# P V of four heads in four column strips, softmax sums from chunks added on GpSimd

## The reference, cut to what matters

```python
# first attention, per batch b
q, k = _rms_norm(q, g_q), _rms_norm(k, g_k)
logits = jnp.einsum('bhqd,bhkd->bhqk', q, k) * d ** (-0.5)
attn = jax.nn.softmax(logits, axis=-1)
o = jnp.einsum('bhqk,bhkd->bhqd', attn, v)
...
# second attention, causal
probs = jax.nn.softmax(scores, axis=-1)
out = jnp.einsum('bhqk,bkhd->bqhd', probs, v).reshape(b, s, H)
return out @ o_w
```

## Time and profile before

| | us |
|---|---|
| three runs | 1286.44, 1295.35, 1297.18 |
| median | 1295.35 |
| the profiled execution | 1290.86 |
| its span | 1289.1 |
| TensorE busy | 1169.7 |
| VectorE busy | 744.4 |
| ScalarE busy | 572.3 |
| GpSimd busy | 290.7 |

### The profile page before, as it was taken

One profiled execution on the slowest core, in us unless ns is written; L12 is line 12 of the kernel. 1 busy time (PEld: TensorE's weight loads), 2 busy tenths in 40 slices (PEclk: granted clock), 3 DMA queues, 4 the chain that ended last, 5 costly groups with the idle time before them and its releaser, 6 DMA issues.

```text
span 1289.1 us, 18670 instructions
## 1 busy us (share of the span) xinstructions
PE 1169.7 (91%) x6059; PEld 825.7 (64%) x6059; DVE 744.4 (58%) x1807; ACT 572.3 (44%) x1248; POOL 290.7 (23%) x244
## 2 busy tenths in 40 slices
PE   5979999999999889999999989989999999999970
PEld 5745555665566446557767757766657888888850
DVE  6565675477545856666565575566364774444433
ACT  3324464345443555455465454455264753222210
POOL 1313122100210031001011200200124464555530
PEclk9979999999999999999999999999899999999995
DMA  7064243125311732352284264265357744555559
GB/s 255 33 180 131 65 136 112 50 86 184 99 50 58 225 107 57 99 189 88 88 259 149 86 234 122 84 201 176 86 186 232 262 152 105 109 108 113 115 134 331
DMA packets 88127, 178.42 MB, mean 138 GB/s; under 512 B 12609, under 2 KB 23265, under 8 KB 86497
## 3 DMA queue, kind: packets, MB, share of 16 engines
q1 hardware_dynamic: 79216, 156.90, 37.4%
q0 software_dynamic: 8512, 19.93, 8.2%
...
...
## 4 chain that ended last, share of the span: by engine, by line
PE 77%; DVE 8%; DMA 5%; ACT 4%; issue 3%; SPq 1%; POOL 0%; DVEq 0%; ACTq 0%; POOLq 0%
PE psum L862 14%; PE psum L681 9%; PE psum L682 8%; PE psum L683 8%; PE psum L846 6%; PE psum L825 6%; PE psum L690 4%; PE psum L940 4%; PE psum L942 4%; PE psum L941 4%; PE psum L967 2%; PE psum L969 2%; PE psum L968 2%; PE psum L909 2%; PE psum L772 2%
## 5 line engine op out<-in xcount | busy, mean ns | idle before, releaser
L1174 ACT ACTIVATE probs<-psum 128x512 f32<-128x512 f32 (+3 forms) x512 | 257.3, 517 | 231.5 <-PE psum L849 120.6
L825 PE MATMUL psum<-stack 96*128 96x512 f32 (+3 forms) x512 | 210.2, 416 | 8.6 <-DMA stack<-split_s 4.0
L1583 DVE TENSOR_REDUCE nmax<-psum 128x1 f32<-128x512 f32 x256 | 170.5, 684 | 77.0 <-PE psum L825 73.2
L846 PE MATMUL psum<-stack 97*128 97x512 f32 (+3 forms) x512 | 197.3, 386 | 16.8 <-ACT probs L1174 15.4
L862 PE MATMUL psum<-probs,vals 128*33 128x512 f32 (+3 forms) x1024 | 209.4, 531 | 0.0
L1586 DVE CUSTOM_DVE_ANT_0 psum<-psum,causal 128x128 f32<-128x128 f32 (+3 forms) x256 | 123.0, 501 | 21.0 <-PE psum L825 19.4
L825 PEld LDWEIGHTS psum<-stack 96*128 96x128 f32 x512 | 100.0, 196 | 46.3 <-issue 23.7
L846 PEld LDWEIGHTS psum<-stack 97*128 97x128 f32 x512 | 99.0, 193 | 40.0 <-ACT probs L1174 25.8
L862 PEld LDWEIGHTS psum<-probs,vals 128*33 128x33 f32 x1024 | 49.8, 112 | 99.6 <-issue 65.5
L681 PE MATMUL psum<-w_hi,xh 128*128 128x512 f32 (+1 forms) x256 | 95.4, 373 | 4.2 <-DVEq L1449 2.5
L682 PE MATMUL psum<-w_hi,xl 128*128 128x512 f32 (+1 forms) x256 | 93.6, 366 | 0.0
...
...
## 6 DMA issues: line engine op xcount, KB each, us to landing
...
```

Source lines behind the costliest of these rows:

```text
L825: sq.filled(nc.tensor.matmul(psum[:, sq.bank(M), 0:n], st[:, 0, t * P:(t + 1) * P], st[:, 1, 0:n], start=True, stop=True), M)
L846: last = nc.tensor.matmul(psum[:, bank, lo:S], st[:, 1, t * P:(t + 1) * P], st[:, 0, lo:S], start=True, stop=not masked)
L1174: sk.cleared(nc.scalar.activation(probs[:, M % NX, lo:S], psum[:, sk.bank(M), lo:S], ACT.Exp, scale=SCALE), M)
L1583: sq.cleared(V.tensor_reduce(out, psum[:, sq.bank(M), :], AX.X, ALU.max, negate=True), M)
```

## The change

`VW`, the 33rd column and the pair's way back are gone. V is 32 columns wide, and `pv(Q, t)` issues, for four heads (a quad, 16 steps) and one chunk t, four products to partitions 0, 32, 64 and 96 of bank 7. The groups stand at steps 11, 12, 14 and 16 of the quad. GpSimd adds chunks 1 to 3 of each head onto the head's chunk 0, in place, after chunk 0 has been used (`add_probs`, at steps 11 to 19). At step 22 TensorE multiplies the four totals by a 128x32 block of ones, which repeats each sum on the 32 partitions of its head (`sum`). VectorE transposes that in 32x32 blocks, takes one reciprocal per query, transposes it back broadcast, and multiplies the P V bank by it into the sum's ring bank (`sum` in the VectorE list); ScalarE and VectorE split the result as before (`o`). There are 14 chunk slots, given out by a table (`SLOT`), and ScalarE waits for the last reader of the slot: a P V group and an add, or the ones product for chunk 0. `out` moves from steps 23 to 35 to 10 to 19 of the next block, the first `qk` from step 3 to 0, the others and `v` too; x1, residual and accumulator rows move in tiles of 128 tokens through a buffer of two tiles.

```diff
 NSTEPS = NB * STEPS_H
 LEAD = 16
 TURN_AHEAD = 5
-LAG = 2
-GROUP = 4
-NX = 2 * GROUP
+NX = 14
+PV_STEPS = (11, 12, 14, 16)
+SUM_STEP = 22
+ADDS = {11: ((0, 1), (1, 1)), 13: ((2, 1), (3, 1)), 14: ((0, 2), (1, 2)), 16: ((0, 3), (1, 3)), 17: ((2, 2), (3, 2)),
+        19: ((2, 3), (3, 3))}
+TAIL_STEPS = 8
...
     if i >= 0:
-        put((5,), [("back", i, NPR - 1)])
-        put((8,), [("turn_o", i, NC - 1)])
-        put((23, 27, 31, 35) if phase(j) == 1 else (25, 29, 33, 37), each("out", i, NT))
+        put((6,), [("sum", i, NQD - 1)])
+        put((8,), [("o", i, NQD - 1)])
+        put((10, 13, 17, 19), each("out", i, NT))
         if phase(i) == 2:
+            put((12, 15, 21, 23), each("acc", i, NT))
             put((28, 33, 36, 41), each("square2", i, NT))
             put((43, 43, 44, 44), each("norm2", i, 4))
-            put((47, 47, 49, 49), each("scale2", i, NT))
-            put((51, 52, 54, 55), each("x2", i, NC))
+            put((46, 46, 47, 47), each("scale2", i, NT))
+            put((49, 51, 52, 53), each("x2", i, NC))
             put((59, 62), each("router", i, 2))
...
     if j < NB and phase(j) == 1:
-        for n, m in enumerate((17, 18, 20, 21, 23, 24, 26, 27) if k == 0 else (3, 5, 7, 11, 13, 15, 19, 21)):
+        for n, m in enumerate((17, 18, 20, 21, 24, 25, 26, 27) if k == 0 else (0, 2, 4, 9, 12, 15, 20, 24)):
             put((m, m + 2), [("qk", j, n), ("hsum", j, n)])
-        put((30, 31, 32, 33) if k == 0 else (24, 25, 26, 27), each("hnorm", j, 4))
-        put((26, 30, 33, 39) if k == B - 2 else (39, 47, 55, 59), each("v", j, NT))
+        put((30, 31, 32, 33) if k == 0 else (27, 28, 29, 30), each("hnorm", j, 4))
+        put((26, 29, 32, 37) if k == B - 2 else (29, 32, 45, 52), each("v", j, NT))
         for g in range(NG):
-            late = 3 if k == 0 and g == 0 else 0
-            put((28, 29) if g == 0 and k else (33, 34) if g == 0 else (30 + 8 * g, 31 + 8 * g), hscales(j, g))
+            late = (3 if k == 0 else 2) if g == 0 else 0
+            put((33, 34) if g == 0 and k == 0 else (31, 32) if g == 0 else (30 + 8 * g, 31 + 8 * g), hscales(j, g))
             put((32 + 8 * g + late, 34 + 8 * g + late), turns(j, g))
     elif j < NB:
-        put((2, 5), [("kv_d", j), ("q_d", j)])
-        for n in range(2 * NT):
-            put((9 + 2 * n, 10 + 2 * n), [("qk", j, n), ("rope", j, n)])
-        put((27, 31, 35, 39), each("v", j, NT))
+        put((0, 2), [("kv_d", j), ("q_d", j)])
+        for n, m in enumerate((4, 9, 12, 15, 21, 24, 26, 28)):
+            put((m, m + 1), [("qk", j, n), ("rope", j, n)])
+        put((30, 33, 36, 45), each("v", j, NT))
         for g in range(NG):
             put((32 + 8 * g, 34 + 8 * g), turns(j, g))
...
         put((60, 61, 62, 63), each("x", after, NC))
-    put(range(13, 64, STEPS_P), each("back", k, NPR - 1))
-    put((38, 46, 57), each("turn_o", k, NC - 1))
+    put(range(SUM_STEP, 64, STEPS_Q), each("sum", k, NQD - 1))
...
+def step_of(Q, head, t):
+
+    return STEPS_Q * Q + STEPS_P * (head // 2) + 2 * t + head % 2
+
+
+def quad_part(M):
+
+    Q, m = divmod(M, STEPS_Q)
+    return Q, m // STEPS_P * 2 + m % 2, m % STEPS_P // 2
...
+def slots_of_probs():
+
+    add_step = {head_t: m for m, parts in ADDS.items() for head_t in parts}
+    slot_of, last, free_at = [], [None] * NX, [0] * NX
+    for M in range(NSTEPS):
+        s = min(range(NX), key=lambda n: free_at[n])
+        Q, head, t = quad_part(M)
+        slot_of.append((s, last[s]))
+        last[s] = (Q, head, t)
+        free_at[s] = STEPS_Q * Q + (SUM_STEP + 1 if t == 0 else max(PV_STEPS[t], add_step[head, t] + 1))
+    return slot_of
+
+
+SLOT = slots_of_probs()
...
         probs = rest("probs", [P, NX, S])
-        vals = [rest(f"vals{n}", [P, NT, H, VW]) for n in range(2)]
+        vals = [rest(f"vals{n}", [P, NT, H, DH]) for n in range(2)]
         vs = rest("vs", [P, 2, S])
         stack = rest("stack", [P, 2, NSTK, S], F32R)
+        spread = at("inverse_sums", rest.where, [P, NC, S])
         oh, ol = rest("o_hi", [P, NC, S], F32R), rest("o_lo", [P, NC, S], F32R)
-        oc = rest("o_chunk", [P, 2, NT, P])
-        ev = rest("o_pair", [P, 2, S])
...
-        yt = rest("yt", [P, NT, D])
+        ones_h = rest("ones_for_sums", [P, DH])
+        yt = rest("yt", [P, 2, D])
...
+            def store_x1(i, t):
+                ring.wait_read(sp, ("out", i, t))
+                sp.dma_start(x1_s[i][:, t, :], yt[:, t % 2, :]).then_inc(y1_st[t % 2], 16)
...
+                    if i >= 0 and phase(i) == 1 and m in (13, 16, 20, 22):
+                        store_x1(i, (13, 16, 20, 22).index(m))
+                    if i >= 0 and phase(i) == 2 and m in (14, 17, 24, 26):
+                        store_acc(i, (14, 17, 24, 26).index(m))
+                    if i >= 0 and phase(i) == 2 and m == 50:
                         store_x2(i)
...
-                elif kind == "back":
-                    p, = at_
-                    o.wait_read(pe, NPR * j + p)
+                elif kind == "sum":
+                    g, = at_
+                    Q = NQD * j + g
+                    pe.wait_ge(s_add, max(ADD_NO[Q, head, NT - 1] for head in range(HPG)) + 1)
                     ring.wait_free(pe, key)
-                    for t in range(NT):
-                        last = nc.tensor.transpose(psum[:, ring.bank(key), t * P:t * P + OW],
-                                                   ev[0:OW, p % 2, t * P:(t + 1) * P], ident[0:OW, 0:OW])
+                    for head in range(HPG):
+                        last = nc.tensor.matmul(psum[DH * head:DH * head + DH, ring.bank(key), :], ones_h[:, :],
+                                                probs[:, SLOT[step_of(Q, head, 0)][0], :], start=True, stop=True)
                     ring.filled(last, key)
-                elif kind == "turn_o":
-                    c, = at_
-                    for p in (2 * c, 2 * c + 1):
-                        ring.wait_read(pe, ("back", j, p))
-                    turn(key, lambda t: oc[:, c % 2, t, :])
                 elif kind == "out":
                     t, = at_
                     if t == 0:
-                        for c in (NC - 2, NC - 1):
-                            ring.wait_read(pe, ("turn_o", j, c))
+                        for g in (NQD - 2, NQD - 1):
+                            ring.wait_read(pe, ("sum", j, g))
...
-            def pv(M):
-                k, h, t = head_step(M)
-                p, side = M // STEPS_P, h % 2 * HALF
-                if M % STEPS_P == 0:
-                    o.wait_free(pe, p)
-                if M % STEPS_H == 0:
-                    for n in (NT - 2, NT - 1):
-                        ring.wait_read(pe, ("v", k, n))
-                sk.wait_read(pe, M)
+            def pv(Q, t):
+                k, g = divmod(Q, NQD)
+                if t == 0:
+                    pe.wait_ge(o_ok, Q)
+                    if g == 0:
+                        for n in (NT - 2, NT - 1):
+                            ring.wait_read(pe, ("v", k, n))
                 lo = t * P if phase(k) == 2 else 0
-                nc.tensor.matmul(psum[side:side + VW, o.bank(p), lo:S], vals[k % 2][:, t, h, :], probs[:, M % NX, lo:S],
-                                 start=(t == 0), stop=(t == NT - 1)).then_inc(pv_mm, 1)
+                for head in (HPG - 2, HPG - 1):
+                    sk.wait_read(pe, step_of(Q, head, t))
+                for head in range(HPG):
+                    nc.tensor.matmul(psum[DH * head:DH * head + DH, O_BANK, lo:S], vals[k % 2][:, t, HPG * g + head, :],
+                                     probs[:, SLOT[step_of(Q, head, t)][0], lo:S],
+                                     start=(t == 0), stop=(t == NT - 1)).then_inc(pv_mm, 1)
 
...
-            for M in range(NSTEPS + LAG):
+            for M in range(NSTEPS + TAIL_STEPS):
...
-                if (M - LAG) % GROUP == GROUP - 1 and M > LAG:
-                    for n in range(GROUP):
-                        pv(M - LAG - GROUP + 1 + n)
-                if M < NSTEPS:
                     for key in BESIDE[M // STEPS_H].get(M % STEPS_H, ()):
                         if key in RING_NO:
                             beside(key)
+                if pv_group(M) is not None:
+                    pv(*pv_group(M))
...
-                elif kind == "turn_o":
-                    c, = at_
-                    if j == 0 and c == 0:
-                        act.wait_ge(spare_set, 3 * 16)
-                    if j and c == 0:
-                        ring.wait_full(act, ("out", j - 1, NT - 1))
-                    hi_of(key, oh[:, c, :])
+                elif kind == "o":
+                    g, = at_
+                    act.wait_ge(o_ok, NQD * j + g + 1)
+                    copy(oh[:, g, :], psum[:, ring.bank(("sum", j, g)), :]).then_inc(hi_ok, 1)
...
-                if M >= NX:
-                    act.wait_ge(pv_mm, M - NX + 1)
+                slot, was = SLOT[M]
+                if was:
```

(75 more changed lines are left out.)

138 lines of the change are left out of this document (81 added, 57 removed).

## The result

The changed kernel takes 1385.3 us (median of 4 runs, 1382.7 to 1387.9) against 1295.3 of the kernel before on the same chip: ratio 1.071, interval 1.066 to 1.076. It is 90 us slower where I had forecast 41 faster. The profiled execution spans 1382.9 us, its mean granted TensorE clock is 0.90 against 0.97.

What follows compares the result with a forecast made beforehand. It took TensorE's order of work to bound the blocks, with GpSimd nearly free. 1290.9 - 98.9 + 23.5 + 22 + 5 + 7 + 5 = 1254.5, said as 1254 us; range 1197 to 1305, the forecast's own 1232 to 1275.

Steps and rivals of the forecast that it cites:

- P V, 88.7 us: P V groups on TensorE: four strips at once, full group 0.99 us for 1.84, 194.6 to 105.9 us, gain 88.7.
- The two-strip rival: Every P V and ones group: only two strips ever run at once, a group stays 1.84 us; 1346 us, chance 0.16.
- the partial one: P V groups: four strips slow one another in part, full group 1.2 to 1.35 us; 1270 to 1300 us, chance 0.07.
- The turns, 44.8: TensorE in the blocks: turns back of pairs (64 x 0.48 = 30.7 us) and of O's chunks (32 x 0.44 = 14.1) go.
- the 98.9 of the sum: TensorE's net saving in us: P V and turns less ones products; 14.7 in each early block, 10.0 in each causal one.
- Ones products, 34.6: Added TensorE work: 32 groups shaped like a full P V group, 0.99 us and 0.09 of entry each, 34.6 us.
- the 45.5 charged: TensorE's waits for late GpSimd: 23.5 us for sums in blocks 0 to 3, 22 at block borders and block 0's step 17.
- the one on the shared port: VectorE scales of xt or heads waiting for GpSimd adds: some 12 a block, 0.4 us each, 20 us, not the bound.
- the 7 above: The 7 us charged in all for VectorE's 2.3 us division bursts, since three score banks cover only two steps.
- The clock, 5 us: TensorE's clock falling behind long gaps: 5 us charged for three gaps.
- The division, 12 us (7 and 5): VectorE's division per quad: 7 us for its bursts, 5 for "out" waiting on O's split in four causal blocks.
- The rival that lateness spreads: Late adds hold probability slots, or VectorE's burst is at its upper bound; TensorE follows; 1270 to 1305 us, chance 0.10.

Runs made afterwards that it cites:

- write_only: Changed kernel with each GpSimd addition replaced by two fills of the same chunk, which read nothing (sums wrong): 1310.2 us, ratio 1.013.
- before_gaps: Kernel before, with 24 gaps in which TensorE waits for five GpSimd fills, at every eighth step of blocks 0 to 2: 1397.8 us, ratio 1.084.
- narrow_early: Changed kernel with additions 8 columns wide (sums wrong) and the division's quotient written to SBUF, freeing the ring's bank two steps earlier: 1259.7 us, ratio 0.975.
- narrow_no_division: Changed kernel with additions 8 columns wide and the division replaced by one VectorE copy (results wrong): 1241.6 us, ratio 0.960.

## Why the prediction was wrong, step by step

- **P V, 88.7 us.** Right. Full group 0.996 us for 0.99, four strips without loss; counted at the full clock P V fell from 194 to 105 us in the blocks. The two-strip rival and the partial one are out. The Trainium skill, "TensorE: Matmul & The Clock Gate", Part 3, has 2.38x for three column tiles; the 1.2 us that I had estimated for a group from it does not show here. The start and end in program order, which that page has too ("What overlaps and what doesn't"), delay no strip here: the four products of a group start within 0.02 us of one another.
- **The turns, 44.8, were mis-sized.** I took 0.48 and 0.44 us from single steps of the chain. In TensorE's own order the next product starts 0.33 us behind the first turn of a pair, and 0.36 behind the first of a chunk. At the full clock all turns of O in the blocks were 32 us. The other products cost 7.5 us more than before (mask products and turns of q and k most of it), for a cause that was not tested. So the work fell by 82 us, not by the 98.9 of the sum. (The split of the 98.9, too, should read 14.9 and 9.8 a block.)
- **Ones products, 34.6.** 36.7 busy, 30.7 at the full clock: right within 4 us.
- **GpSimd.** Durations right (1.28, 1.01, 0.735 against 1.303, 1.013, 0.746). Its waits were placed right: xl at the borders of blocks 1 and 2 5.9 us each for 7, at step 17 of block 0 6.6 for 8, sums 12.2 for 23.5. A wait for w_lo in block 3 (7.9) had no term of its own; with it that is 39 of the 45.5 charged.
- **The step that failed most is the one on the shared port.** I wrote "Some 12 such operations a block, 0.4 each, in four blocks are 20 us of VectorE that is not the bound; they sit in the 7 above." Three things in it are wrong. The number: I counted the wide scales and forgot the refining steps, 18 chained operations an early block, all with two SBUF operands, and the first guesses in front of them. The price: 0.42 in the earlier trace rows was the rest of one operation that happened to be running; against additions back to back it is nearly a whole addition each, 0.16 to 0.29 us becoming 0.54 to 1.42. The wide scales that I had counted hardly grew (xt 0.54 to 0.63, q and k 0.70 to 0.77). Together VectorE worked some 81 us more (its 117 less 36 for the division) instead of 20, 58 of them in the refining steps. And the judgement that it is not the bound: the row maxima queue behind these operations, and TensorE runs only three score banks ahead. The price in time is 75 us (write_only), 43 for the refining steps alone.
- **The clock, 5 us.** 71 more were lost by it than before. I charged three gaps; the blocks have fifty of 1 to 8 us (16 in the kernel before), and before_gaps shows that each costs its length and, at 3.2 us, 1.8 more. So the clock comes on top of the idle time of every other error, here 71 us on 98.
- **The division, 12 us (7 and 5).** VectorE's added time was right: transposes 0.71 for 0.69. But leaving the division out gives 46 us, 23 of which are the bank of the ring that sums, quotient and O's low part hold for two steps. The prediction had no term for that bank, though it named waits on the division as a sign of being wrong.
- **Causal blocks.** Forecast 10 shorter each, measured 1 to 7 longer, 406.2 us together. With narrow additions they are as long together as before (390.9 against 388.3 us), and 365.2 without the division too: there the division and its bank weigh more (26 us) than the additions (15).
- **The rival that lateness spreads** (1270 to 1305) does not explain it either: ScalarE waits 3.4 us for additions, not long, and the transposes were never slow. Only its picture of VectorE's work holding up TensorE is right, and its time is 80 us too short at the least.

What stays open: narrow_early has neither additions nor the held bank, and takes 1260, while my terms without GpSimd give 1290.9 - 98.9 + 5 + 7 = 1204. Of these 56 us 17 are the work term. In its trace TensorE is idle in the blocks 26 us longer than before and loses 24 more by the clock, where I had charged 12 for the division. 25 us of its waits are for row maxima (3.5 before). Whether they come from the division's time on VectorE or from the moved steps was not tried: without division and additions (narrow_no_division) TensorE still idles 71 us for 53 and loses 35 by the clock for 14.
